# Two buffers for the pair sums, and a gather queue that waits for VectorE's sums and for transposes two chunks back

## What is computed

```python
# block 1: 1x1 conv to 128 channels, a 3x3 depthwise conv whose kernels are
# generated from the image's own mean, mish, 1x1 conv back to 64
x = x + conv1x1(mish(depthwise3x3(xh, kernels(mean(xh)))))      # xh = conv1x1(gn(x))
# block 2: deformable 3x3 conv
offset = conv3x3(gn(x), w_off); mask = sigmoid(conv3x3(gn(x), w_mask))
# per output pixel and tap k: four neighbours of a fractional position, weighted bilinearly, times mask
val[k] = sum_of_4(gathered_corner[k] * weight[k])
xd = einsum('bikhw,oik->bohw', val, w_def)
x = x + silu(batchnorm(conv1x1(concat(xd, offset, mask))))
```

## Time and profile before

| | |
|---|---|
| median of three runs | 6789.73 us |
| the profiled execution | 6784.49 us |
| its span, first to last instruction | 6782.7 us |
| DVE busy | 4588.9 us (68%) |
| POOL busy | 4394.7 us (65%) |
| PE busy (matmuls) | 3546.7 us (52%) |
| ACT busy | 1702.1 us (25%) |
| mean granted TensorE clock | 0.678 of full speed |

### The profile page before, as it was taken

How to read it: one execution, slowest core, us unless ns; L and a number is a source line. 1 busy time by engine, 2 the same in 40 slices (tenths; PEclk the granted TensorE clock), 3 DMA queues, 4 the chain that set the end, 5 groups by cost and what they waited for, 6 DMA issues and landing times.

```text
span 6782.7 us, 30330 instructions
## 1 busy us (share of the span) xinstructions
PE 3546.7 (52%) x8724; PEld 1333.6 (20%) x8724; DVE 4588.9 (68%) x4403; ACT 1702.1 (25%) x2555; POOL 4394.7 (65%) x4614
## 2 busy tenths in 40 slices
PE   8655474554645546465564654547455464554422
PEld 3221121211212112121121221112121121211100
DVE  5776767677676676667767676676767667667555
ACT  3322222322222222222222222222232222222100
POOL 2666666666666666666666666666666666666666
PEclk8766676766767667666666766667666676766655
DMA  3233343333433334333343333333333343333332
GB/s 90 87 99 113 95 118 94 104 111 95 116 95 106 106 100 115 95 102 108 101 114 91 106 109 101 110 96 109 101 103 113 93 119 95 105 102 100 100 99 88
DMA packets 306958, 695.44 MB, mean 103 GB/s; under 512 B 79172, under 2 KB 148580, under 8 KB 304548
## 3 DMA queue, kind: packets, MB, share of 16 engines
q0 software_dynamic: 221184, 604.27, 29.7%
q1 hardware_dynamic: 85606, 89.22, 5.3%
HBM read 639.06 MB, written 54.12 MB: 102 GB/s over the span
## 4 chain that ended last, share of the span: by engine, by line
DVE 34%; another core or an unknown queue 28%; issue 12%; PE 11%; POOL 8%; ACT 6%; DMA 0%; ACTq 0%; DVEq 0%; POOLq 0%; SPq 0%
DVE pairs L1042 12%; DVE gat L1057 10%; POOL gat L379 8%; PE om_ps L517 3%; PE yo_ps L517 2%; PE z_ps L551 2%; DVE tr_ps L933 2%; DVE om_ps L933 2%; DVE single L1042 2%; DVE xb L956 1%; DVE stat L958 1%; DVE stat L891 1%; DVE uc L940 1%; DVE uc L946 1%
## 5 line engine op out<-in xcount | busy, mean ns | idle before, releaser
L379 POOL DMA_INDIRECT gat<-patch_table,ixu x4608 | 4387.1, 952 | 2370.5 <-issue 1354.9
L1042 DVE TENSOR_REDUCE pairs<-gat 128x256 f32<-128x1024 f32 x1024 | 1938.7, 1893 | 0.0
L1057 DVE TENSOR_TENSOR gat<-gat,wgt_ps 128x1024 f32<-128x1024 f32 x1152 | 1394.6, 1213 | 549.7 <-DMA gat<-patch_table,ixu 500.5
L551 PE MATMUL z_ps<-val,w_pair 128*64 128x512 f32 x1024 | 888.0, 965 | 909.6 <-ACT val L784 703.4
L543 PE MATMUL tap_ps<-ident,pairs 128*128 128x128 f32 x2048 | 475.4, 374 | 1514.5 <-issue 1015.8
L784 ACT ACTIVATE val<-tap_ps 128x512 f32<-128x512 f32 x512 | 299.1, 596 | 2956.1 <-remote 2147.2
L543 PEld LDWEIGHTS tap_ps<-ident,pairs 128*128 128x128 f32 x2048 | 316.9, 188 | 1921.0 <-issue 1316.0
L933 DVE SCALAR_TENSOR_TENSOR tr_ps<-xh,kb,tr_ps 128x512 f32<-128x512 f32 x186 | 139.6, 750 | 445.2 <-remote 434.9
L517 PE MATMUL om_ps<-np,w_om 128*41 128x512 f32 x732 | 380.7, 676 | 0.0
L517 PE MATMUL yo_ps<-np,w_om 128*41 128x512 f32 x804 | 367.4, 607 | 6.0 <-ACT omc L740 6.0
L551 PEld LDWEIGHTS z_ps<-val,w_pair 128*64 128x64 f32 x1024 | 137.0, 190 | 1067.6 <-ACT val L784 739.8
(11 more groups left out here) (176 smaller groups left out, 3534.2 us busy)
## 6 DMA issues: line engine op xcount, KB each, us to landing
gat<-patch_table,ixu POOLq DMA_INDIRECT x4608
xb<-in_x SPq DMA_DIRECT2D x31, 1024.0 KB
patch_table<-rec SPq DMA_DIRECT2D x120, 256.0 KB
out<-n_z SPq DMA_DIRECT2D x128, 128.0 KB
patch_table<-np SPq DMA_DIRECT2D x2, 1072.5 KB
patch_table<-gat SPq DMA_DIRECT2D x8, 256.0 KB
patch_table<-rec_l SPq DMA_DIRECT2D x16, 97.0 KB
xb<-in_x SPq DMA_DIRECT2D x2, 512.0 KB, 5.3
```

What stands on the lines that cost most here:

```text
L379: pool.indirect_dma_start(gat[:, slot, t * 2 * REC:(t + 1) * 2 * REC], None, table_rows, bass.IndirectOffsetOnAxis(ixu[:, i, k, t:t + 1], ...
L551: pe.matmul(z_ps[0:C, :], w_pair[:, p, :], val[:, p % 2, :], start=(p == 0), stop=False).then_inc(z_mm, 1)
L1042: dve.tensor_reduce(total, gat[:, slot(q, k), :].rearrange("p (t d c) -> p t c d", t=TILES, d=4), mybir.AxisListType.X, ALU.add).then_inc( ...
L1057: dve.tensor_tensor(patch, patch, wk.unsqueeze(2).to_broadcast([128, TILES * 4, C]), ALU.mult).then_inc(scaled, 1)
```

## The change

`pairs` and `single` get two buffers, chunks using them in turn (`q % 2`). To make room, `cat` shrinks to two chunks (2 x 512) and the offset and mask rows move to a new `cat_om` (128 x 4096), in which even and odd images lie in different partitions; ACT copies each chunk's part from there into `cat` ahead of the chunk's first pair, one more activation of 41 x 512 a chunk. POOL's five waits on `tap_mm` become one, at tap 0, for all transposes of chunk q-2, and four waits on `summed` at taps 0, 2, 4 and 6: for 2, 4, 6 and 8 sums of chunk q-1.

```diff
-THROTTLE = {0: 1, 2: 2, 4: 3, 6: 4, 7: 5}
+SLOTS = {0: 2, 2: 4, 4: 6, 6: 8}
-        cat = sb("cat", [128, 2, PIX])
+        cat_om = sb("cat_om", [128, PIX])
+        cat = sb("cat", [128, 2, CH])
-        pairs = sb("pairs", [128, PAIRS, TILES, 2 * C])
-        single = sb("single", [128, TILES // 2, 2 * C])
+        pairs = sb("pairs", [128, 2, PAIRS, TILES, 2 * C])
+        single = sb("single", [128, 2, TILES // 2, 2 * C])
+        def om_rows(n):
+            return cat_om[C * (n % 2):C * (n % 2) + OM, :]
                         for k in range(KK):
-                            if k in THROTTLE:
-                                pool.wait_ge(tap_mm, q * GROUPS + THROTTLE[k])
+                            if k == 0 and q > 1:
+                                pool.wait_ge(tap_mm, q * GROUPS)
+                            if k in SLOTS and q > 0:
+                                pool.wait_ge(summed, q * KK + SLOTS[k])
...
-                    pe.matmul(z_ps[0:C, :], w_last[:, :], cat[0:C + OM, b % 2, span(g)], start=False, stop=True).then_inc(z_mm, 1)
+                    pe.matmul(z_ps[0:C, :], w_last[:, :], cat[0:C + OM, q % 2, :], start=False, stop=True).then_inc(z_mm, 1)
...
-                act.activation(cat[C:C + OM, n % 2, bass.ds(s * (2 * CH), 2 * CH)], omc[:, :, :].rearrange("p j c -> p (j c)"), ACT.Copy).then_inc(cat_done, 2)
+                act.activation(om_rows(n)[:, s * 2 * CH:(s + 1) * 2 * CH], omc[:, :, :].rearrange("p j c -> p (j c)"), ACT.Copy).then_inc(cat_done, 2)
...
+                if lo == 0:
+                    act.wait_ge(cat_done, q + 1)
+                    act.activation(cat[C:C + OM, q % 2, :], om_rows(b)[:, g * CH:(g + 1) * CH], ACT.Copy)
```

More of the change, by code:

```diff
@@ L542, in transposes @@
                 for t in range(TILES if p < PAIRS else TILES // 2):
-                    m = pe.transpose(tap_ps[p % 2][:, t * 128:(t + 1) * 128], pairs[:, p, t, :] if p < PAIRS else single[:, t, :], ident[:, :])
+                    m = pe.transpose(tap_ps[p % 2][:, t * 128:(t + 1) * 128], pairs[:, q % 2, p, t, :] if p < PAIRS else single[:, q % 2, t, :], ident[:, :])
                 m.then_inc(tap_mm, 1)
@@ L756, in first_pixels @@
                 act.wait_ge(om_done, q + 1)
-                act.activation(cat[C:C + OM, n % 2, span(c)], omc[:, c % 2, :], ACT.Copy).then_inc(cat_done, 1)
+                act.activation(om_rows(n)[:, c * CH:(c + 1) * CH], omc[:, c % 2, :], ACT.Copy).then_inc(cat_done, 1)
             def indices(q):
@@ L787, in sample @@
                         for h in range(2):
-                            act.activation(cat[0:C, b % 2, span(g)].rearrange("p (t h x) -> p t h x", h=2, x=128)[:, :, h, :],
+                            act.activation(cat[0:C, q % 2, :].rearrange("p (t h x) -> p t h x", h=2, x=128)[:, :, h, :],
                                            tap_ps[PAIRS % 2][C * h:C * h + C, 0:CH // 2].rearrange("p (t x) -> p t x", x=128), ACT.Copy).then_inc(tap_done, 1)
@@ L1039, in add_corners @@
                 p, half = k // 2, k % 2
-                total = pairs[:, p, :, half * C:half * C + C] if p < PAIRS else single[:, :, :].rearrange("p t (h c) -> p (t h) c", h=2)
+                total = pairs[:, q % 2, p, :, half * C:half * C + C] if p < PAIRS else single[:, q % 2, :, :].rearrange("p t (h c) -> p (t h) c", h=2)
                 dve.wait_ge(scaled, q * KK + (k + 1))
```

## The result

The changed kernel takes 7944.91 us (median of four runs, 7938.18 to 7952.21) beside 6790.83 us for the kernel before: ratio 1.17, interval 1.168 to 1.1721. It is slower by 1154 us. The forecast was 7110 us with a range up to 7520: the sign held, the size did not.

The account below looks back on a forecast made before the run. POOL's own work was taken as 85% of the span, the rewritten waits worth 878 us at most. 6784.5 + 324 (other terms 0) = 7108, with 5 us for the median 7114, rounded to 7110 us; range 6350 to 7520.

Parts of the forecast that it names:

- ACT's copies and the buffers: ACT's 128 added copies fall where ACT idles, and the buffers add no PE or DVE instructions: cost 0, or 80 us uncovered.
- The mechanism: After some 24 us of unbroken gathers PE's results are held up; a POOL pause of about 6 us releases them.
- The pause at tap 4: POOL runs 16 gathers further, then waits for six sums; its pause grows from 6.4 to 17.7 us, the chunk to 62.8.
- VectorE's idle time before the convolution: A sign the forecast is right: DVE idles near 29 us before L933, in chunks where it is 9 now.
- ACT's wait: A sign the forecast is right: "remote" waits of ACT's `val` copies become longer than 23 us.
- How often: Chunks 0 to 3, images 0 to 14: one third lose 11.3 us, two thirds 2.5; +324 us, bounds 150 and 680.
- the prediction's last sign: If POOL pauses at a chunk's first gather, the wait for chunk q-2 has taken the place of the old one.
- Chunks 4 to 7: POOL running ahead helps DVE, fewer pauses delay PE's offset passes; taken as 0, bounds -150 to +300 us.
- The last image: Treated together with chunks 4 to 7, gain set against loss: 0 us taken.
- Rivals 1 to 3: PE unslowed, 5912 us, chance 0.06; stall halved, 6250 to 6770, chance 0.26; pause only moved, 6780 to 6800, chance 0.08.
- the forecast's own case: Slower: POOL's 16 more gathers keep PE stuck; 6784 to 7764 us with its low and high ends, chance 0.60.

Follow-up runs that it names:

- e1: The changed kernel with POOL's five old waits for PE put back, buffers and ACT's copies kept: 6780.95 us, ratio 1.0004 to the kernel before.
- e3: The changed kernel, waits unaltered, with POOL filling a 128x768 scratch tile ten times at the head of every chunk: 7511.95 us, ratio 1.109 to the kernel before.
- e12: A separate kernel of only PE transposes and ACT copies, without or beside POOL's gathers or plain loads: 19 groups in 119.8 us beside gathers, 57 in 100 beside loads.
- e7: The changed kernel with one 128x768 scratch fill by POOL ahead of every tap, nine a chunk: 6733.43 us, ratio 1.001 to the kernel before.
- e5: The changed kernel with POOL waiting for PE's transposes of the chunk before at taps 0 and 4: 6760.98 us, ratio 1.0043 to the kernel before.
- e13: The changed kernel with one 128x640 scratch fill by POOL ahead of every tap: 7034.25 us, ratio 1.045 to the kernel before.
- e14: The changed kernel with e13's fills and e5's two waits for PE: 6710.37 us, ratio 0.9978 to the kernel before.
- e16: e12's transposes and copies beside 96 gathers, with fills of several sizes: longest result delay 9.4 us at 1.25 us a gather, 0.7 at 1.41.
- stretch 4: The part of e12 with POOL's gathers and six 512-column matmuls ahead of every transpose group: 3 groups came through, results 28 to 38 us late.

## Why the prediction failed in size

- **ACT's copies and the buffers: nothing.** Right. ACT's busy time rose by 80 us (1702 to 1782 in e1) and the time by less than 0.13%.
- **The mechanism** (POOL's pause lets PE go, and waiting for PE makes POOL pause in time). Right in what mattered, shown by e3 and e12. Wrong in one detail, that it takes a pause of some 6 us: nine rests of 0.6 us do as well, as e7 shows. The 5.8 us between POOL's last gather and PE's results are real (5.9 in the chunk above), but no pause of that length is needed.
- **The pause at tap 4.** Forecast 17.7 us, a chunk of 62.8. Measured 16.6 to 16.9 in chunks 3 and 4, a chunk of 61.4, and 18.8 in chunk 2, released by VectorE's sum at the 17th gather as described. VectorE's idle time before the convolution was put at 29 us; it was 14.0 + 9.1, as the first pass came through alone. ACT's wait of 35.5 us is above the 23 of before.
- **How often.** I gave a third of chunks 0 to 3 the long pause and so +324 us. Measured +338. That is luck in part: chunks 2 and 3 have it in every image (+11.9 and +9.9 us). Chunk 0 is 7.2 us longer for another reason, the 14.1 us ahead of the first gather of chunk 1, and within chunk 1 there is no pause (45.0, -6.6). That pause is the case of the prediction's last sign, the wait for two chunks back in place of the old one; it is 102 us in all.
- **Chunks 4 to 7: this step failed.** I took 0, bounds -150 and +300. It was +820: 10, 9, 18 and 17 us a chunk. I set a gain against a loss, since the trace had "no row for the balance". The gain was there but small: VectorE's waits for gathers fell by 256 us. The loss isn't a matter of busy time, and it has two parts. Chunk 4's 10 us, some 150 us in all, are the very pause at tap 4 that I had priced for chunks 0 to 3: POOL gathers ahead of the others, so the convolution that stands in chunk 3's plan stops it in chunk 4 (16.7 us, and VectorE waits 12.7 + 10.5 us in that convolution). My count of the chunks went by the plan. The rest falls in chunks 5 to 7. There PE passes its results to ACT, ACT back to PE, PE to VectorE, and VectorE's indices to POOL, one after the other, and each hand-over through PE can meet the hold-up. It shows at VectorE's wait for the transposed offsets (264 to 731 us before L1008) and at POOL's for the indices (451 us). That the hold-up makes them late is shown by e5, where one more rest in the middle of the chunk takes chunks 5 to 7 from 60, 73 and 62 us to 54, 52 and 49; how much each hand-over adds is not shown. A hint stood in the earlier trace rows: 159 waits "remote" of 5 us on average are more than one for each of 128 chunks. In the trace of the kernel before POOL pauses two or three times in chunks 5, 6 and 7, where PE has most to do, and once in chunks 1 to 4.
- **The last image: nothing.** Right, 1 us less.
- **The rivals.** Rivals 1 to 3 are out. e1 shows that the waits alone make the difference; the runs with fills show why so little was to be won. With gathers 50.7 / 36 = 1.41 us apart PE is on time in chunks 1 to 5 and the time is that of the kernel before (e7, 1.001), at 1.38 us it is 4.5% longer (e13), and the best mix of fills and waits gains 0.2% (e14). The kernel before took 51.5 us a chunk there, 1.43 us a gather: hardly any of its 878 us of waits was there to be taken.
- **The range** ended at 7520 while the forecast's own case, with both high ends, stood at 7764 in the text. Even that was 181 us short: it allowed 680 us for chunks 0 to 3, where 338 came, and 300 for chunks 4 to 7, where 820 came.

## What to carry to other kernels

Before a wait is taken off an engine, ask what else its idle time does: put the same idle time back without the wait (a fill of a scratch tile), and see whether the gain of the removal or its loss depends on the wait at all. A stage that hands results back and forth between engines pays a delay once for each hand-over, so price it along that chain and not by busy time. Where the text says that no row shows a term, and that term covers half of the kernel, the range has to be that wide.

## What the runs showed of the hardware

- POOL's indirect gathers of 128 rows, issued every 1.25 us, slow PE down to 4 transposes in 11.2 us; at 1.41 us they don't (e12, e16). At 1.25 us the first late result came 21 us after the first gather (e12). Half the bytes change nothing (e4: 1.168 beside 1.170), and 96 plain loads in 100 us do nothing (e12: 123 GB/s beside 104). In stretch 4, with six 512-column matmuls and four transposes a group, a group took 41 to 46 us. What in the chip links the two engines stays open: no run here separates what POOL does when it issues a gather, and no view separates late work of PE from late signals of it. The Trainium skill, SBUF — State Buffer, "Who interferes with whom", has PE wait for no one; the section is about SBUF's ports. e12 shows that it can't be read as a rule for PE beside gathers from POOL.
- In e12 every second gather took about 1.65 us instead of 0.95 while VectorE worked on operands in SBUF alone; in the full kernel, where VectorE's second operand is in PSUM, they stay at 0.95. The same section of the Trainium skill says that a VectorE instruction with two inputs in SBUF contends with a GpSimd instruction that reads SBUF; the 0.7 us agree with that. These gathers stood 1.6 us apart and PE was on time, as e16 has it for 1.41 us; that VectorE's work could free PE in this way was not expected.
